# VectorE in place of ACT copies z and the conv's input out of PSUM in a fused Mamba and feed-forward kernel

## What is computed

```python
x = x + layernorm(mamba(layernorm(x)))
x = x + layernorm(ffn(layernorm(x)))

def mamba(x):                                   # d_inner 512, state N = 16, dt_rank 16
    h = x * rsqrt(mean(x * x) + eps) * norm_w
    u, z = split(h @ in_proj_w.T)
    uc = silu(conv_b + sum(up[:, k:k + L] * conv_w[:, k] for k in range(4)))   # causal, over tokens
    dt, Bm, Cm = split(uc @ x_proj_w.T)
    dt = softplus(dt @ dt_proj_w.T + dt_proj_b)
    # h_t = exp(dt * A) * h_{t-1} + dt * Bm * uc ;  y_t = sum over the 16 states of h_t * Cm
    y = (y + uc * D) * silu(z)
    return y @ out_proj_w.T + x

def ffn(x):                                     # hidden 1024
    h = silu(x @ w1 * s1) * (x @ w2 * s2)
    h = gelu(h @ h1 * sh1)
    h = gelu(h @ h2 * sh2)
    return h @ w3 * s3
```

## Time and profile before

| | |
|---|---|
| time, median of 3 runs | 1962.97 us (1961.39 to 1963.79) |
| the profiled execution | 1959.91 us, its span 1958.1 us |
| mean granted TensorE clock | 0.842 of full speed |
| busy: PE, DVE, ACT, POOL | 1469.4, 1318.2, 1242.6, 1182.5 us |
| ACT's copies of z and u (L915, L921) | 32 and 32 instructions, 18.6 and 18.8 us |
| TensorE waits for z's copy (L600) | 42.0 us, 13 times |
| DMA | mean 33 GB/s, busy a tenth or less after the weights are in |

### The profile page before, as it was taken

How to read it: one execution, slowest core, us unless ns; L and a number is a source line. 1 busy time by engine, 2 the same in 40 slices (tenths; PEclk the granted TensorE clock), 3 DMA queues, 4 the chain that set the end, 5 groups by cost and what they waited for, 6 DMA issues and landing times.

```text
span 1958.1 us, 30115 instructions
## 1 busy us (share of the span) xinstructions
PE 1469.4 (75%) x9080; PEld 1282.1 (65%) x9080; DVE 1318.2 (67%) x1962; ACT 1242.6 (63%) x2622; POOL 1182.5 (60%) x1503
## 2 busy tenths in 40 slices
PE   4666678877777877877777878887787877876864
PEld 2222567767776777776776777776776777775764
DVE  2678876867668676867668676877668676866310
ACT  4454576767576676667577676758577676766443
POOL 1634657666657567676657667676667657666322
PEclk8787888888888888888788988888888987887977
DMA  3222100101001010101001010101001010000000
GB/s 109 97 81 70 33 23 18 41 23 35 20 23 40 18 37 23 40 18 40 19 18 41 23 36 24 34 24 34 25 18 40 24 35 24 29 23 29 2 7 6
DMA packets 38934, 63.76 MB, mean 33 GB/s; under 512 B 5216, under 2 KB 19424, under 8 KB 38640
## 3 DMA queue, kind: packets, MB, share of 16 engines
q10 hardware_dynamic: 18944, 33.83, 5.8%
q1 hardware_dynamic: 19696, 26.02, 4.1%
HBM read 55.38 MB, written 4.46 MB: 31 GB/s over the span
## 4 chain that ended last, share of the span: by engine, by line
PE 30%; POOL 28%; issue 17%; ACT 12%; DVE 10%; POOLq 1%; ACTq 1%; DVEq 0%; DMA 0%; SPq 0%
POOL S L468 16%; PE fP L612 8%; PE fP L613 7%; POOL Glo L539 5%; PE sT L636 5%; DVE S L1118 4%; PE hP L600 3%; PE fP L600 3%; ACT dA L865 2%; DVE acc L1132 2%; PE fP L733 2%; PE fP L734 2%; POOL S L471 1%; POOL x L549 1%; ACT Rw L1028 1%
## 5 line engine op out<-in xcount | busy, mean ns | idle before, releaser
L468 POOL TENSOR_TENSOR S<-X,Bs 128x1024 f32<-128x1024 f32 x256 | 610.0, 2383 | 374.6 <-PE sT L636 271.2
L1118 DVE TENSOR_TENSOR_SCAN S<-dA,S 128x512 f32<-128x512 f32 x512 | 621.3, 1214 | 172.9 <-ACT dA L865 106.9
L865 ACT ACTIVATE dA<-delta,A 128x255 f32<-128x255 f32 x1024 | 446.8, 470 | 423.9 <-DVE S L1118 261.2
L612 PE MATMUL fP<-Ghi,w_h 128*128 128x256 f32 x2048 | 567.0, 312 | 117.8 <-POOL Glo L539 80.1
L613 PE MATMUL fP<-Glo,w_h 128*128 128x256 f32 x2048 | 539.2, 298 | 0.0
L612 PEld LDWEIGHTS fP<-Ghi,w_h 128*128 128x128 f32 x2048 | 427.5, 209 | 138.0 <-POOL Glo L539 72.6
L1132 DVE SCALAR_TENSOR_TENSOR acc<-sT,CT,acc 128x512 f32<-128x512 f32 x480 | 350.4, 733 | 202.3 <-PE sT L636 201.6
L636 PE MATMUL sT<-ident,S 128*128 128x128 f32 x2048 | 354.6, 306 | 117.9 <-DVE acc L1132 101.7
L613 PEld LDWEIGHTS fP<-Glo,w_h 128*128 128x128 f32 x2048 | 427.7, 209 | 0.0
L636 PEld LDWEIGHTS sT<-ident,S 128*128 128x128 f32 x2048 | 269.6, 157 | 190.1 <-DVE acc L1132 103.3
L539 POOL TENSOR_TENSOR Glo<-Rw,Ghi 128x1024 fp32r<-128x1024 f32 x96 | 225.8, 2354 | 194.4 <-ACT Ghi L1035 179.9
(11 more groups left out here) (137 smaller groups left out, 2036.2 us busy)
## 6 DMA issues: line engine op xcount, KB each, us to landing
Bs<-b_rows ACTq DMA_DIRECT2D x128, 256.0 KB, 3.1
Rw<-in_h SPq DMA_DIRECT2D x11, 512.0 KB, 3.2
xh<-in_x SPq DMA_DIRECT2D x16, 256.0 KB, 2.8
xt<-in_x SPq DMA_DIRECT2D x16, 256.0 KB, 2.9
out<-x SPq DMA_DIRECT2D x16, 256.0 KB, 2.2
x<-in_h SPq DMA_DIRECT2D x5, 512.0 KB, 3.2
Rw<-in_w SPq DMA_DIRECT2D x4, 512.0 KB, 4.6
w_in<-in_in_proj SPq DMA_DIRECT2D x1, 1024.0 KB, 5.7
```

The source lines that it names most:

```text
L468: pool.tensor_tensor(s[:, :, :], X[par][:, :, :], row[:, None, :].broadcast_to([P, DT, T]), ALU.mult).then_inc(scan_pool.sem, 1)
L612: pe.matmul(dst, w[:, i, cols_], hi[:, i, :], start=(j == 0), stop=False)
L865: a = act.activation(dA[half][:, i, 1:], delta[par][:, d, 1:], ACT.Exp, scale=A[:, d * N + n:d * N + n + 1])
L1118: a = dve.tensor_tensor_scan(pair, dA[half][:, :, :].rearrange("p d t -> p (d t)"), pair, 0.0, ALU.mult, ALU.add)
```

## The change

The copies of z (half steps 11 and 12) and of u (13 and 14) go from ACT's program to VectorE's, as `tensor_copy`, and with them the steps that others wait for. VectorE's list has the halo copy two half steps later, at 12, behind z's second copy. In half step 14 the head's part stands ahead of `gather` on VectorE. The head's statistics go from half step 3 to 1. GpSimd's program and the DMA queues are unchanged.

```diff
         head_vec = Steps(sem("head_vec"),
-                         ["x_stats", "x_aggr", "halo", "tap0", "tap1", "tap2",
+                         ["x_stats", "x_aggr", "z0", "z1", "halo", "u0", "u1", "tap0", "tap1", "tap2",
                           "t1", "res", "log1p", "delta"])
         head_act = Steps(sem("head_act"),
-                         ["hn", "hT", "z0", "z1", "u0", "u1", "cbase", "silu0", "silu1",
+                         ["hn", "hT", "cbase", "silu0", "silu1",
...
-                        pe.wait_ge(head_act.sem, head_act.at(h, ("z0", "z1")[q - 2]))
+                        pe.wait_ge(head_vec.sem, head_vec.at(h, ("z0", "z1")[q - 2]))
...
-                if hs in (11, 12):
-                    q = hs - 11
-                    if q == 0:
-                        act.wait_ge(tail_pe.sem, tail_pe.at(h - 2, "out"))
-                    act.wait_ge(head_pe.sem, head_pe.at(h, f"z{q}"))
-                    act.copy(z[hp][:, 2 * q:2 * q + 2, :], hP[(q + 1) % 2][:, :, :]).then_inc(head_act.sem, 1)
-                if hs in (13, 14):
-                    q = hs - 13
-                    if q == 0:
-                        act.wait_ge(head_vec.sem, head_vec.at(h, "halo"))
-                    act.wait_ge(head_pe.sem, head_pe.at(h, f"u{q}"))
-                    act.copy(u_ext[:, 2 * q:2 * q + 2, CONV - 1:], hP[(q + 1) % 2][:, :, :]).then_inc(head_act.sem, 1)
                 if hs == 14:
-                    act.wait_ge(head_act.sem, head_act.at(h, "u1"))
+                    act.wait_ge(head_vec.sem, head_vec.at(h, "u1"))
...
             def head_step(h, hp, hs, first):
-                if hs == 3:
+                if hs == 1:
                     dve.wait_ge(xh_in.sem, xh_in.at(h, "landed"))
                     stats(head_vec, h, ("x_stats", "x_aggr"), xh, hstat, hmv)
-                if hs == 10:
+                if hs in (11, 12):
+                    q = hs - 11
+                    if q == 0:
+                        dve.wait_ge(tail_pe.sem, tail_pe.at(h - 2, "out"))
+                    dve.wait_ge(head_pe.sem, head_pe.at(h, f"z{q}"))
+                    dve.tensor_copy(z[hp][:, 2 * q:2 * q + 2, :], hP[(q + 1) % 2][:, :, :]).then_inc(head_vec.sem, 1)
+                if hs in (13, 14):
+                    q = hs - 13
+                    if q == 0:
+                        dve.wait_ge(head_vec.sem, head_vec.at(h, "halo"))
+                    dve.wait_ge(head_pe.sem, head_pe.at(h, f"u{q}"))
+                    dve.tensor_copy(u_ext[:, 2 * q:2 * q + 2, CONV - 1:], hP[(q + 1) % 2][:, :, :])\
+                       .then_inc(head_vec.sem, 1)
+                if hs == 12:
                     ahead, last = u_ext[:, :, 0:CONV - 1], u_ext[:, :, T:T + CONV - 1]
...
                     if scan:
                         back(c, par, n, hs % 2)
+                    if head and hs == 14:
+                        head_step(c + 1, 1 - par, hs, None)
...
-                    if head:
+                    if head and hs != 14:
```

More of the change, by code:

```diff
@@ L975, in silus @@
                                        ACT.Silu).then_inc(head_act.sem, 1)
-                    act.wait_ge(head_act.sem, head_act.at(h, "z1"))
+                    act.wait_ge(head_vec.sem, head_vec.at(h, "z1"))
                     act.activation(z[hp][:, :, :], z[hp][:, :, :], ACT.Silu).then_inc(head_act.sem, 1)
```

## The result

The changed kernel takes 1959.12 us (median of 20 runs, 1954.29 to 1960.97), against 1963.34 for the kernel before in the same series (20 runs). The ratio is 0.9978 [0.9967, 0.9988]: 4.3 us faster, just over the 0.2% that the prediction took for what a measurement can tell. I had forecast 11.3. The sign and the range hold, the size does not.

A forecast was written before the change was run, and what follows sets the result against it. The prediction took a ring of engines waiting for each other, none full, to bound the kernel. Its terms, -10.4 - 3.4 + 2.5 = -11.3 us, taken from 1962.97, gave 1952 us, with a range of 1938 to 1963.

The forecast's parts named there:

- What bounds the kernel: No engine is full; engines wait for each other, longest GpSimd for the turned state on TensorE.
- the ring: Circle of engines waiting for each other; a microsecond saved on an engine counts only where it stands on this circle.
- A: Halo copy from half step 10 to 12: seven stalled bodies start their Gelu earlier, -10.4 us (bounds -12 to -6).
- B: Second Gelu's table load (T) to ACT's copy of the w3 product: -3.4 us in all, bounds -19 to +0.5.
- low clock: Rival: TensorE between u and first branch products, one more stretch at 1.2 GHz, 1.4 us per body, 1970; chance 0.08.
- C: VectorE's copies out of PSUM: covered in the loop, charged in prologue and first bodies, +2.5 us (bounds 0 to +6).
- D: Head's statistics from half step 3 to 1 on VectorE: fits in a gap, cost in the loop 0.
- The range: Forecast span of the time, 1938 to 1963 us, from middle of the high-clock case to top of the no-difference case.
- The sign of being wrong that I had named: TensorE's mean granted clock, 0.842, moving by more than 0.01 would show the prediction wrong.
- High clock: Rival: w3 runs at 2.4 GHz throughout, -27 us, 1936; chance 0.12.
- No copy out of PSUM waited for GpSimd: Answers a rival: VectorE's PSUM copies wait behind GpSimd's products, 2.8 us per body, half exposed, 1970; chance 0.03.
- No difference: Rival: early Gelu at half step 11 doesn't come, or the halo stall returns where it costs; 1959 to 1963, chance 0.12.

The follow-up runs named there:

- the run with the low parts first: Changed kernel with GpSimd's two low parts of Gelu made one after the other in half step 12, ahead of its next scan work: 1904.21 us.
- both moves and ACT's copies: Kernel before with halo copy in half step 12 and statistics in half step 1, ACT keeping the four PSUM copies: 1950.76 us.

## Why the prediction was wrong in size

**What bounds the kernel**: right. The Glo chain and w3 behind it are on the ring; the run with the low parts first, 55 us, shows it.

**A, the halo copy**: right in mechanism, 10.4 forecast. In the traces G to T fell by 9.8 us, and the move alone gave 8.4. The sentence that even a full stall at half step 12 would end before ACT wants the next scan is what the halo copy alone showed, in all 12 bodies that have both a halo copy and a second Gelu. In the changed kernel the two z copies ahead of it push it out of the race altogether.

**B, from table load to w3's end**: here the prediction failed. Its starts were right to a tenth of a us: Ghi at T+5.5, w3's second part at T+14.0 (measured 13.94). The clock was mis-sized. I took 18.4 us as the new stretch, "near the slow end", between 17.2 and 18.7, and measured 19.4 on average, above my upper bound. That bound took body 10 as the slowest case, but its 0.61 is a mixture: its first 8 products, up to 1228.5, had a granted clock of 1.00, the other 16 of 0.50. The slowest case is 24 products at 0.21 us, 5.1 us, plus 0.45 to the copy. In place of -3.4 us came +10.3. I had seen the longer idle time ahead of w3's second part (about 4 us; measured 2.8 to 3.6, and 1.96 more ahead of the first part) and the low clock was even a rival, but I put it at 0.08 and took the new stretch inside the range of the old ones. I counted the u products that no longer start cold as a point against the low clock. They were the opposite: they had taken the low clock on themselves, where it was covered, and now w3 has it in every body (granted 0.50 to 0.57). T to O averages 19.4 us against 18.6 before.

**C, what VectorE pays**: the copies took 0.69 us as forecast. Up to w3 they are covered: its second part starts at T+13.9 in every body. Whether they cost anything in the rest of the loop isn't shown; G to T is 554.0 us against 550.4 with both moves and ACT's copies. I had 2.5 us for the start; there the trace shows -0.8, for the whole change.

**D, the statistics**: forecast 0, measured -3.9 alone and about -2 in the whole change, which is within the noise there. I looked for their cost in the loop and found none, rightly. I did not look at body 0, where 1 us of VectorE's time decides a race with GpSimd.

**The range** held by luck: with B as measured my sum is -10.4 + 10.3 + 2.5 = +2.4 us, and that the kernel is faster all the same is owed to terms that I had wrong or not at all (the start, the statistics, O to G). The sign of being wrong that I had named did come: the mean granted clock moved by 0.014, from 0.842 to 0.828.

**The rivals**: low clock had the right place and nearly the right price. I made it cost 18 us, 1.4 a body, on top of A and B; against my -3.4 it cost 13.7, 1.05 a body, just under the 1.2 from which I had put the kernel down as slower. High clock came in no body. No copy out of PSUM waited for GpSimd: all 64 lie between 666 and 693 ns, and 42 of them ran beside a GpSimd instruction of over 1 us. No difference has the measured time in its range, but its reason did not come: the Gelu's load is early in every body.

## What to carry to other kernels

- When a wait in front of TensorE goes, ask where its idle time goes. Here its amount stayed (66.5 and 68.7 us in 13 stretches), but it moved from in front of covered products to around exposed ones, and the low clock moved with it. Bound such a stretch by all its products at 1.2 GHz, not by the slowest body seen.
- A stall costs only where someone waits for it: halo copies of 19.5 us, nearly all under the Gelus, cost nothing that G to T shows, and those of 17.8 us two half steps earlier cost 8. Before buying engine time, look at which engine's queue holds the two halves of one product's input apart. Here the order of two GpSimd steps was worth 55 us, the change under study 4.
- Products that keep TensorE busy are sure to pay only in time it would have idled. The same 20 took 30 us off one kernel and added 43 to another. With 34 on the path, in a third kernel, what the clock gave elsewhere still left a gain of 14: try it, and read both stretches.

## What the runs showed of the hardware

- 22 products with a weight of 8 columns kept the granted clock at 1.00 as well as products of 128 columns did.
- A VectorE product of 128x1024 with both inputs in SBUF, 1.23 us, took 3.38 when GpSimd's product had started 0.04 us before. A GpSimd step of 0.2 us took 1.2 when it was second. VectorE's copies of 128x512 from PSUM, 42 of 64 of them beside GpSimd instructions of over 1 us, never waited.
- A w3 part wholly at 1.2 GHz has its products 0.213 us apart, one at 2.4 GHz 0.12, or 0.11 when it follows other products without a gap.
- Before the change the granted clock fell during w3's second part in the 7 of 13 bodies whose gap ahead of it was 2.05 to 2.23 us, and stayed at 1.00 in the six with 1.22 to 1.96. The gap alone doesn't tell: with the low parts first the clock was low in 8 of 13 bodies, behind gaps of 1.96 us ahead of the first part and 0.5 to 1.1 us between the parts.
